# Layer-normed activations turned by transposing DMA instead of TensorE, and the SyncE queue reordered

## The reference

```python
xn = layernorm(x)                                  # per token, eps 1e-5
Q, K, V = xn @ Wq.T + bq, xn @ Wk.T + bk, xn @ Wv.T + bv
Q, K = elu(Q) + 1, elu(K) + 1
KV = einsum('bshd,bshe->bhde', K, V)
Z = 1.0 / (einsum('bshd,bhd->bsh', Q, K.sum(1)) + 1e-6)
attn = einsum('bshd,bhde,bsh->bshe', Q, KV, Z).reshape(b, s, E) @ Wo.T + bo
probs = softmax(xn @ gate_w)                       # 8 experts
g, m = top_k(probs per expert over the 1024 tokens, 256)
h = gelu(xn[m] @ w1[e]) @ w2[e]                    # per expert, 256 -> 1024 -> 256
ffn = scatter_add(g * h).astype(bfloat16)
return x + attn + ffn
```

## Time and profile before

| | |
|---|---|
| median of 3 runs | 2110.74 us (2110.18 to 2111.15) |
| the profiled execution | 2120.3 us, span 2118.6 us |
| mean granted TensorE clock | 0.986 of full speed |
| PE busy over the span | 1992.9 us (94%) |
| DVE busy | 1401.2 us (66%) |
| ACT busy | 1248.1 us (59%) |
| POOL busy | 883.3 us (42%) |
| the 32 TensorE transposes x 16 passes, L1157 | 50.2 us busy |
| their copies on ACT, L734 | 75.7 us busy |

### The profile page before, as it was taken

One profiled execution on the slowest core, in us unless ns is written; L12 is line 12 of the kernel. 1 busy time (PEld: TensorE's weight loads), 2 busy tenths in 40 slices (PEclk: granted clock), 3 DMA queues, 4 the chain that ended last, 5 costly groups with the idle time before them and its releaser, 6 DMA issues.

```text
span 2118.6 us, 41289 instructions
## 1 busy us (share of the span) xinstructions
PE 1992.9 (94%) x14240; PEld 1365.3 (64%) x14240; DVE 1401.2 (66%) x2836; ACT 1248.1 (59%) x1975; POOL 883.3 (42%) x776
## 2 busy tenths in 40 slices
PE   3899999999999799999999999999999999999984
PEld 2566666667667666666666666666666666666653
DVE  5877888788876467776557777555555555555535
ACT  3765555556655265666565656665666666666642
POOL 2122212221221345555555545455555555454632
PEclk9999999999999899999999999999999999999997
DMA  4555454434443445555566666666666757666676
GB/s 152 176 169 179 150 186 148 133 109 139 128 148 110 112 100 126 124 134 115 126 148 161 163 162 160 152 172 154 169 166 158 177 147 178 152 173 152 171 196 189
DMA packets 379375, 321.17 MB, mean 152 GB/s; under 512 B 155013, under 2 KB 360842, under 8 KB 379274
## 3 DMA queue, kind: packets, MB, share of 16 engines
q1 hardware_dynamic: 312842, 236.00, 37.9%
q0 software_dynamic: 49152, 67.14, 17.0%
q10 hardware_dynamic: 17280, 16.78, 2.4%
HBM read 185.61 MB, written 100.66 MB: 135 GB/s over the span
## 4 chain that ended last, share of the span: by engine, by line
PE 52%; POOL 4%; DMA 3%; DVE 2%; SPq 2%; issue 2%; ACT 1%; POOLq 0%; ACTq 0%; DVEq 0%
PE pY L1681 26%; PE pH L1667 26%; POOL acc L1507 2%; SPq L223 2%; DMA stage<-in_w 2%; DMA xg<-table,idx 1%; POOL xg L217 1%; DVE yo L1582 1%; DVE hid L1569 0%; ACT hid L1527 0%; ACT gel L1524 0%; DMA acc<-yo,idx 0%; DVE w2s L205 0%; DVE lmix L1600 0%; ACT w2s L197 0%
## 5 line engine op out<-in xcount | busy, mean ns | idle before, releaser
L1681 PE MATMUL pY<-w2s,hid 128*128 128x256 f16 x6144 | 756.8, 273 | 16.1 <-DVE hid L1569 15.9
L1667 PE MATMUL pH<-xgT,w1s 128*128 128x512 f16 x3072 | 750.4, 381 | 4.3 <-PEq L319 4.3
L1681 PEld LDWEIGHTS pY<-w2s,hid 128*128 128x128 f16 x6144 | 600.0, 98 | 200.0 <-DVE hid L1569 21.5
L1507 POOL DMA_INDIRECT acc<-yo,idx x256 | 418.3, 1634 | 548.9 <-DVE yo L1582 490.4
L1569 DVE SCALAR_TENSOR_TENSOR hid<-gel,cur,hid 128x512 f16<-128x512 f32 x512 | 382.7, 747 | 369.7 <-ACT hid L1527 360.4
L1524 ACT ACTIVATE gel<-pH,cur 128x512 f32<-128x512 f32 x512 | 349.8, 683 | 386.6 <-PE pH L1667 378.4
L1667 PEld LDWEIGHTS pH<-xgT,w1s 128*128 128x128 f16 x3072 | 301.3, 98 | 261.0 <-issue 9.1
L1527 ACT ACTIVATE hid<-gel,cur 128x512 f16<-128x512 f32 x512 | 369.7, 722 | 16.7
L217 POOL DMA_INDIRECT xg<-table,idx x256 | 284.5, 1111 | 113.6 <-issue 61.0
L1169 PE MATMUL pP<-wkv,xT 128*128 128x512 f16 x768 | 191.1, 386 | 0.0
L672 POOL TENSOR_TENSOR x2ring<-x2ring,bo_all 128x512 f32 (+1 forms) x64 | 85.3, 1363 | 141.5 <-DMA x2ring<-in_x 141.5
(11 more groups left out here) (185 smaller groups left out, 2095.3 us busy)
## 6 DMA issues: line engine op xcount, KB each, us to landing
stage<-in_w SPq DMA_DIRECT2D x160, 512.0 KB, 4.8
xring<-in_x SPq DMA_DIRECT2D x16, 1024.0 KB, 6.6
x2ring<-in_x SPq DMA_DIRECT2D x16, 1024.0 KB, 8.3
table<-xhl SPq DMA_DIRECT2D x32, 512.0 KB, 3.9
acc<-zeros SPq DMA_DIRECT2D x16, 1024.0 KB, 6.7
mix<-x2ring SPq DMA_DIRECT2D x32, 512.0 KB, 2.8
fmix<-mix SPq DMA_DIRECT2D x48, 256.0 KB, 5.8
facc<-acc SPq DMA_DIRECT2D x48, 256.0 KB, 6.6
```

The costliest lines, as they stand in the source:

```text
L1507: g.indirect_dma_start(acc, bass.IndirectOffsetOnAxis(ap=idx[q][:, s:s + 1], axis=0), yo[i][:, s, :], None, compute_op=ALU.add).then_inc(a ...
L1667: last = t.matmul(pH[hc % 4][:, :], w[:, aw, c, hc * P:(hc + 1) * P], xgT[i][:, ad, c, :], start=k == 0 and c == 0, stop=k == 2 and c == D ...
L1681: last = t.matmul(pY[s // 2][:, s % 2, :], hid[:, hc % 4, ad, s * P:(s + 1) * P], w[:, aw, hc, :], start=hc == 0 and k == 0 and s % 2 == 0 ...
```

## The change

- `turn` leaves PE, and `turn_out` leaves ACT. SP now issues for each tile one transposing DMA from `xhl` to `xT`, with a semaphore per tile, `x_turned[j]`. PE's `project` waits for it, and ACT's `high` waits for it before it overwrites `xhl`.
- SP's turn of a tile waits for `lo_done`, and at tiles 0 and 4 also for the `q_part` of the batch before, which reads the same half of `xT`.
- SP's pass is put in a new order, shown below.
- The first group's probabilities are turned in one step of four transposes in slot 3 into a bank of their own, with one DVE copy in slot 4, and PE no longer waits for the copy.

The diff, cut to what the prediction speaks of:

```diff
-            pTK = ps("pTK", [P, 2, 2 * DC * P], F16)
-            pT = pTK[:, 0, :].rearrange("p (a c t) -> p a c t", a=2, c=DC)
-            pK = pTK[:, 1, :].bitcast(F32)
+            pK = ps("pK", [P, 512])
...
-            turned = event("turned", per=NT, credit=HALF + 1)
-            xT_done = event("xT_done", per=NT, credit=1)
+            x_turned = [event(f"x_turned{j}", step=16, credit=1) for j in range(NT)]
...
-                def body(n, s1, s2, load, load2, scan):
+                def turn(n, j):
+                    h, jj = divmod(j, HALF)
+                    value = held(sp, at(lo_done, n, j))
+                    sp.wait_ge(consts, 1)
+                    sp.wait_ge(lo_done, value)
+                    if jj == 0 and not (isinstance(n, int) and n == 0):
+                        value = held(sp, at(q_proj, n - 1, 2 * h + 1))
+                        sp.wait_ge(consts, 1)
+                        sp.wait_ge(q_proj, value)
+                    sp.dma_start_transpose(
+                        xT[h][:, :, :, jj * P:(jj + 1) * P].rearrange("p a c t -> p (a c) t"),
+                        xhl[h][:, jj, :, :, :].rearrange("p a c t -> p (a c t)")).then_inc(x_turned[j], 16)
+
+                def store_rows(n, h):
...
+                def store_mix(m, h):
...
+                def body(n, s1, s2, load, load2, scan, nxt):
+                    m = n - LAG
+                    if s1:
+                        turn(n, HALF)
+                        store_rows(n, 0)
                     if scan:
                         pieces(n, range(2))
                     if load:
...
                         sp.dma_start(xring[:, (n + 2) % XR, :, :], x_rows[ds(n + 2, 1)].rearrange("o p j d -> p (o j) d")).then_inc(x_in, 16)
                     if s1:
+                        turn(n, HALF + 1)
+                    if load2:
+                        value = held(sp, at(x2_in, m))
...
+                        sp.dma_start(x2ring[:, ds((m + 1) % 2, 1), :, :].rearrange("p o j d -> p (o j) d"),
+                                     x_rows[ds(m + 1, 1)].rearrange("o p j d -> p (o j) d")).then_inc(x2_in, 16)
+                    if s1:
+                        turn(n, HALF + 2)
+                        turn(n, HALF + 3)
+                        store_rows(n, 1)
+                    if scan:
+                        pieces(n, range(2, PIECES))
+                    if nxt:
+                        turn(n + 1, 0)
+                        turn(n + 1, 1)
+                    if s1:
                         sp.dma_start(
                             acc_rows[ds(n, 1)].rearrange("o p j d -> p (o j) d"),
                             zeros[:, :].unsqueeze(1).to_broadcast([P, NT, D])).then_inc(zero_out, 16)
...
+                    if nxt:
+                        turn(n + 1, 2)
                     if s2:
+                        store_mix(m, 0)
+                    if nxt:
+                        turn(n + 1, 3)
+                    if s2:
+                        store_mix(m, 1)
+
+                for j in range(HALF):
+                    turn(0, j)
...
                     if jj == 0:
                         act.wait_ge(row_out[h], at(row_out[h], n, -1))
-                        act.wait_ge(turned, at(turned, n, j + HALF - 1 - NT))
+                        for i in range(HALF):
+                            act.wait_ge(x_turned[j + i], at(x_turned[j + i], n, -1))
...
-                def turn_out(n, j):
...
-                def turned_probs(step):
+                def turned_probs():
                     lanes = slice(0, 2 * rows_of(0))
-                    dve.wait_ge(p_turned, at(p_turned, step))
-                    v.tensor_copy(rows[lanes, step * 256:(step + 1) * 256], pK[lanes, :]).then_inc(rows_done, 1)
+                    dve.wait_ge(p_turned, at(p_turned, 0))
+                    v.tensor_copy(rows[lanes, :], pK[lanes, :]).then_inc(rows_done, 1)
...
-                def turn(n, j):
...
                 def project(n, j):
                     h, jj = divmod(j, HALF)
-                    pe.wait_ge(xT_done, at(xT_done, n, j))
+                    pe.wait_ge(x_turned[j], at(x_turned[j], n))
...
                     for j in range(NT):
-                        if prep and j in (4, 5):
-                            pe.wait_ge(rows_done, at(rows_done, j - 4))
-                        if s1:
-                            if j < NT - 1:
-                                turn(n, j + 1)
-                            elif nxt:
-                                turn(n + 1, 0)
...
-                        if prep and j in (3, 4):
+                        if prep and j == 3:
                             pe.wait_ge(prob_done, at(prob_done, PREP - 1, 1))
-                            pe.wait_ge(xT_done, at(xT_done, n, j + 1))
-                            turn_probs(pe, 0, pK, (2 * j - 6, 2 * j - 5))
+                            turn_probs(pe, 0, pK)
```

More of the change, by code:

```diff
@@ L225, in turn_rows, with turn_probs @@
                     xg[i][:, s, :, :, :].rearrange("p a c t -> p (a c t)")).then_inc(xT_in[i], 16)
-        def turn_probs(pe, k, bank, tiles):
-            for t, jl in enumerate(tiles):
-                last = nc.tensor.transpose(bank[0:2 * rows_of(k), t * P:(t + 1) * P], probs[:, jl, lane_cols(k)], ident[:, :])
+        def turn_probs(pe, k, bank):
+            for jl in range(HALF):
+                last = nc.tensor.transpose(bank[0:2 * rows_of(k), jl * P:(jl + 1) * P], probs[:, jl, lane_cols(k)], ident[:, :])
             last.then_inc(p_turned, 1)
@@ L534, in body @@
                     if s1:
+                        turn(n, HALF + 1)
+                    if load2:
+                        value = held(sp, at(x2_in, m))
+                        sp.wait_ge(consts, 1)
+                        sp.wait_ge(x2_in, value)
                         for h in range(2):
-                            value = held(sp, at(lo_done, n, (h + 1) * HALF - 1))
+                            value = held(sp, at(mix_out[h], m, -1))
                             sp.wait_ge(consts, 1)
[L538 to L546, removed]
+                            sp.wait_ge(mix_out[h], value)
+                        sp.dma_start(x2ring[:, ds((m + 1) % 2, 1), :, :].rearrange("p o j d -> p (o j) d"),
[10 more added lines that the diff above has]
+                    if s1:
                         sp.dma_start(
@@ L549, in body @@
                             zeros[:, :].unsqueeze(1).to_broadcast([P, NT, D])).then_inc(zero_out, 16)
[L550 to L559, removed]
-                    if s2:
[L561 to L570, removed]
+                    if nxt:
+                        turn(n + 1, 2)
+                    if s2:
+                        store_mix(m, 0)
[5 more added lines that the diff above has]
+                    turn(0, j)
                 for lo, hi, s1, s2, load, load2, scan in [
@@ L583, in _ @@
                                 sp.dma_start(staged(r), part_src(0, r)).then_inc(part_in[r], 16)
-                        body(lo, s1, s2, load, load2, scan)
+                        body(lo, s1, s2, load, load2, scan, lo < NB - 1)
                         if lo == NB:
@@ L589, in _ @@
                         with sp.Fori(lo, hi) as n:
-                            body(n, s1, s2, load, load2, scan)
+                            body(n, s1, s2, load, load2, scan, True)
                 value = held(sp, at(zero_out, NB - 1))
@@ L604, in _ @@
                 g = nc.gpsimd
-                for ev in (*row_out, *mix_out, *piece_done, xm_done, veps_done, rstd_done, turned, xT_done, kv_done, k_done, kv_used,
+                for ev in (*row_out, *mix_out, *piece_done, xm_done, veps_done, rstd_done, *x_turned, kv_done, k_done, kv_used,
                            kv_out, gsub_done, q_proj, qraw_done, q_done, shifted, den, kv_turned, qz_done, mix_done,
@@ L1102, in body @@
                                 gate_probs(n, 0)
-                            if n == PREP and j in (3, 4):
-                                turned_probs(j - 3)
+                            if n == PREP and j == 4:
+                                turned_probs()
                             top_slot(n, j)
@@ L1149, in _ @@
                     last.then_inc(wturn, 1)
-                def turn(n, j):
-                    h, jj = divmod(j, HALF)
-                    pe.wait_ge(lo_done, at(lo_done, n, j))
-                    pe.wait_ge(xT_done, at(xT_done, n, j - 1))
-                    for a in range(2):
-                        for c in range(DC):
-                            last = t.transpose(pT[:, a, c, :], xhl[h][:, jj, a, c, :], ident16[:, :])
-                    last.then_inc(turned, 1)
                 def project(n, j):
                     h, jj = divmod(j, HALF)
-                    pe.wait_ge(xT_done, at(xT_done, n, j))
+                    pe.wait_ge(x_turned[j], at(x_turned[j], n))
                     pe.wait_ge(kv_done, at(kv_done, n, j - 2))
@@ L1263, in _ @@
                 pe.wait_ge(whi, at(whi, 0, 4))
```

(3 more changed lines are left out.)

32 lines of the change are left out of this document (20 added, 12 removed).

## The result

The changed kernel took 2129.88 us (median of 9 runs, 2124.38 to 2137.65). The kernel before took 2113.81 us in the 9 runs beside it (2110.18 to 2121.48). The ratio is 1.0074 [1.0061, 1.0088]: slower by 16 us, where 22 were forecast; 2129.88 us lies inside the stated range of 2108 to 2152. The profiled execution took 2131.73 us with a span of 2129.9, 11.3 us more than the span before, and a mean granted clock of 0.967 in place of 0.986.

What follows compares the result with a forecast made beforehand. PE bounds a pass except from the last q_part to slot 3, where DVE sets the pace. Terms -3.6 + 18.6 - 2.7 + 5.2 + 5.0 + 1.2 - 1.8 = +21.9 us, added to 2110.7, gave 2133 us, range 2108 to 2152.

Steps and rivals of the forecast that it cites:

- The hold: DVE's slot 1, passes 0 to 7: waits for the piece behind tile 4's turn; +18.6 us in passes 2 to 7.
- Passes 0 and 1: KV sum and gate scores wait for held DVE: 4.6 + 1.0 less 0.4 = +5.2 us.
- The clock term: Passes 2 to 7: PE idles 5 us before slot 3, its clock falls; 0.8 us each, +5.0 us.
- The term of 1.2 us for a later pass: Passes 8 to 15: one pass with a longer wait may cross into a clock fall; +1.2 us.
- The gain of the late passes: Passes 8 to 15: only turns of tiles 6 and 7 on PE's path; 0.45 us each, -3.6 us.
- Pass 4: PE's two waits for copies of the probabilities go, -1.8 us; turns of tiles 6 and 7 save 0.45 us.
- The turns: Transposing DMAs land within a lead of 10 us; the wait of project for them costs nothing.
- Rival 1: DVE's slot 1, passes 0 to 7: piece not late in effect, kernel faster by 9 to 31 us, nearer 2100; chance 0.15.
- Rival 2: Both sides cancel: landing at 3.4 us, no clock cost, half the zero-cost turns pay; about 2111 us; chance 0.12.
- rival 3: Passes 0 to 7: DMA engines become the bound, the piece lands 3 us later again; 2157 us; chance 0.11.
- rival 4: All 16 passes: turns follow slowly, 1.3 us a block, PE waits for x_turned; about 2300 us; chance 0.02.
- signs that were to prove the prediction wrong: piece does not wait, PE waits for the turns, or late passes shrink by 1 us or more.

Runs made afterwards that it cites:

- e1: Changed kernel with pieces 0 and 1 issued at the head of SP's pass, ahead of tile 4's turn: 2095.34 us, ratio 0.9902.
- e4: Kernel before, turns on PE, with pieces 0 and 1 issued behind tile 4's low part and half the table: 2132.22 us, ratio 1.0095.
- e3: Kernel before, with the x2ring load issued behind tile 6's low part, between the two table stores: 2105.79 us, ratio 0.9958.
- e8: Changed kernel with pieces 0 and 1 first, and turns of tiles 0 to 5 issued twice, the second into an unread tile: 2106.78 us, ratio 0.9959.
- e5: Changed kernel, SP order unchanged, with DVE reading the pieces in slots 3, 4, 6 and 7 instead of 1, 3, 5, 7: 2093.43 us, ratio 0.9884.
- e7: Changed kernel, pieces 0 and 1 first, pieces read in slots 3, 4, 6, 7, plus search steps moved to slots 3 to 7: 2086.51 us, ratio 0.9852.

## Why the prediction was right or wrong

e1 stands between the two kernels: it has everything of the change but the late pieces. So e1 less before is the change's gain, and after less e1 the cost of the hold. Both can be placed by three points of PE's order of time. The first is the start of `denominators` in slot 0 of pass 2, ahead of that pass's hold; before, e1 and after:

```profile
98.03 2.03 PE L1216 MATMUL pQ<-qring,ksz 128*128 x16
...
93.75 2.03 PE L1229 MATMUL pQ<-qring,ksz 128*128 x16
...
102.85 2.03 PE L1229 MATMUL pQ<-qring,ksz 128*128 x16
```

The second is the same in pass 8 (353.81, 338.29 and 374.48 us), the third the start of `reciprocals` in pass 17 (712.31, 687.84 and 723.46 us).

| us | passes 0, 1 | 2 to 7 | 8 on | sum | forecast |
|---|---|---|---|---|---|
| gain (e1 less before) | -4.3 | -11.2 | -9.0 | -24.5 | -0.4 - 4.5 - 3.6 = -8.5 |
| cost (after less e1) | +9.1 | +27.1 | -0.6 | +35.6 | 5.6 + 23.6 + 1.2 = +30.4 |

The table stands for one execution of each kernel, and that of the kernel before was a long one. The whole spans differ by -22.3 and +33.6, since e1's second block is 2 us longer than the others'; the medians differ by -18.5 and +34.5.

- **The hold** was the right mechanism, at the right place, and by the right count. DVE's waits for pieces were 28.5 us against 24.2 forecast; in passes 2 to 7 they were 21.35 against 18.6. In pass 3 the piece came 6.95 us after tile 4's low part (150.75 to 157.70), where the working had 7.1. Passes 2 to 7 cost 27.1 us where hold and clock together were put at 23.6. e1 and e4 show the cause from both sides.
- **Passes 0 and 1** were undersized, 5.6 against 9.1 us. DVE's holds there were 2.84 and 4.33 us, 7.2 in place of 5.6; that of pass 0 had been put at 1. The clock term had been given to passes 2 to 7 alone; yet in pass 0 PE waits 4.12 us for `phik` before 47.86, and over 45 to 60 us the granted clock is 0.89, against 1.00 in e1. In pass 1 it is 0.75 over 76 to 90 us; in e1, over 72 to 86 us, 1.00. That the clock makes up the remaining 1.9 us was not tested by itself.
- **The clock** fell in every pass from 2 to 7, as forecast: 0.50 at 118.5 to 124 us, the level of 1.2 GHz. Over the 6 us from the start of `reciprocals` it was 0.50 to 0.72 in these six passes; in e1 it was 1.00 in passes 2 to 5, and 0.72 and 0.74 in 6 and 7, behind waits of 2.60 and 2.59 us. Of the 27.1 us the holds leave 5.7, near the 5.0 that the clock was given, but what the falls cost was not isolated. The term of 1.2 us for a later pass has no basis: in pass 9 the clock over those 6 us is 0.72 before, in e1 and after alike. Nor does the length of the wait alone decide: 1.94 us in pass 5 of e1 was followed by 1.00, 1.85 us in pass 9 of the kernel before by 0.72.
- **The gain of the late passes** is the step that failed, though the total came inside the range. "Those of tiles 6 and 7 are on the path: 2 x 0.22 = 0.45 us per pass" had the right mechanism and nearly the right size: from e3's 40.13 to e1's 39.55 us in pass 11 is 0.58 us. (In the early passes it is more: passes 2 and 3 take 40.5 us each in e3 and 39.5 in e1.) The sentence that was wrong is "the later x loads and stores move by a few us within passes that wait for none of them: 0". PE and DVE did not wait for the load, but POOL did, 8.92 us in pass 11, and began its additions when it landed; these slow the DVE operations that PE waits for. By the medians, e3 makes this 8.05 of the 18.5 us that e1 gains (by the spans, 8.8 of 22.3). The other 10 to 14 us are left for the turns, pass 4 and the start, put at 8.5; no run takes these three apart.
- **Pass 4** was put at -1.8 - 0.45. From 193.26 to 236.31 it took 43.05 us before, and 184.96 to 225.16, 40.2 us, in e1: -2.85 us. But passes 2 and 3, which never had these copies, lost 1.77 and 2.02 us as well, so the copies' own part may be no more than about 1 us.
- **The turns** are hidden, as forecast: in the changed kernel PE waits for none after the first, and the six more per pass of e8 cost nothing from pass 2 on. The lead of 10 us was more than enough for a landing of 2.8 us (median; the longest was 8.5).
- **Rival 1** (faster, if the piece is in time) names the right condition. e1 and e5 are that case: 2095 and 2093 us, where it gave 2100. Rival 2 (both sides cancel) needed shorter holds than forecast and no cost of the clock; the holds were longer, and the clock fell in all six passes. Rivals 3 and 4 fall for passes 2 on with e8, where PE keeps its pace with 14 turns a pass; for the start, rival 3 stays open. As for rule and trace in rival 4, the turn's four blocks land 2.8 us after issue (median of 128), 0.7 us a block with everything in it, against the 1309 ns a block of the Trainium skill (VectorE: DVE Perf Modes, The three transpose paths); and in the changed kernel PE never waits for a turn after the first.
- The forecast gain was too small by 16 us in the table (10 by the medians) and the forecast cost by 5 (4 by the medians). The two errors pull the total in opposite directions, so it was nearer than its terms, and that part of the closeness is luck. One of the signs that were to prove the prediction wrong did show: the late passes shrank by more than 1 us.

## What to carry to other kernels

A queue that issues in order passes each wait on to everything behind it, so for every transfer that a reordering puts behind a new wait, compare the new issue time plus landing with the moment its reader stands ready; a reader in the critical stream pays in full, and swapping two lines can be worth more than the work removed. When a load moves, ask also whose work it sets off and what that work runs beside, even if the engine that sets the pace never waited for the load. After taking work off the busiest engine, look at the order of the engine it waits for: here moving the search steps out of DVE's first slots (e7) was worth another 9 to 10 us, half of what the change with the pieces first had gained.

## What the runs showed of the hardware

- DVE operations slow down under POOL's additions, but not all. `phik` (0.42 to 1.53 us), the low part (0.46 to 0.82 and 1.23) and `xm` (0.34 to 1.36) do; `qz` and the addition to `x2ring`, whose second input is in PSUM, keep their 0.67 to 0.69 us in the same stretch. The Trainium skill (SBUF — State Buffer, Who interferes with whom) offers the reason: a DVE instruction with two SBUF inputs contends with a GpSimd instruction that reads SBUF, one in a 2-port mode with GpSimd in general, and whoever began first keeps the shared ports for its whole instruction. The trace agrees in kind and size: no delay is above 1.3 us, and POOL's four additions take 5.33/4 = 1.33 us each. No run here tests the reason by itself.
- A 128x512 16-bit transposing DMA within SBUF takes SP 1.19 us to issue (median) and lands 2.8 us after the issue (median of 128; 2.4 to 8.5). Eight per pass raise the DMA engines' busy share over 470 to 509 us from 0.44 before to 0.53 after, which gives an estimate of 0.09 x 39/8 = 0.44 us of all engines each; e8's six more give (0.64 - 0.54) x 39/6 = 0.65 us. The bound taken from the earlier trace rows was 1.9.
